# Post-LN decoder layer: values for eight heads at a time in twelve slots, v2 behind the first cross head, cross keys projected late in the self transposed stage

## The reference, cut to what matters

```python
x = layernorm(x + attn(x, w_qkv, w_proj, q_norm_w, k_norm_w))   # self: RMS norm and rotary on q, k; causal softmax
x = layernorm(x + xattn(x, ctx, ctx, mask, Wq, Wk, Wv, Wo))      # cross: keys and values from ctx, causal too
x = layernorm(x + ffn(x, ...))                                   # heavy (1024) and light (128) gelu branches, added
```

## Time and profile before

| | us |
|---|---|
| median of 3 runs | 953.05 (951.24 to 955.12) |
| the profiled execution, its own time | 952.55 |
| its span, first to last instruction | 950.8 |

### The profile page before, as it was taken

How to read it: one execution, slowest core, us unless ns; L and a number is a source line. 1 busy time by engine, 2 the same in 40 slices (tenths; PEclk the granted TensorE clock), 3 DMA queues, 4 the chain that set the end, 5 groups by cost and what they waited for, 6 DMA issues and landing times.

```text
span 950.8 us, 21384 instructions
## 1 busy us (share of the span) xinstructions
PE 852.0 (90%) x7381; PEld 649.0 (68%) x7381; DVE 720.1 (76%) x1765; ACT 632.8 (67%) x1404; POOL 538.7 (57%) x1047
## 2 busy tenths in 40 slices
PE   3367898999999999999999999999999999889887
PEld 2235565776867677776867676776867676657677
DVE  7788787787888878877888878877888879675522
ACT  1132453787878787787878778787878777776352
POOL 7554464656656574665756575655756665444143
PEclk8769898999999999999999999999999999999999
DMA  3794382845656382736676482826566472823101
GB/s 113 105 179 82 50 108 37 115 48 91 80 102 79 60 111 47 108 41 109 74 102 79 71 104 46 109 37 116 66 102 79 74 97 46 105 34 54 27 2 34
DMA packets 79660, 74.21 MB, mean 78 GB/s; under 512 B 8608, under 2 KB 78912, under 8 KB 79552
## 3 DMA queue, kind: packets, MB, share of 16 engines
q1 hardware_dynamic: 75024, 68.11, 50.7%
q10 hardware_dynamic: 4528, 4.73, 1.9%
HBM read 17.49 MB, written 4.20 MB: 23 GB/s over the span
## 4 chain that ended last, share of the span: by engine, by line
PE 60%; DVE 21%; ACT 5%; issue 5%; POOL 4%; DMA 3%; SPq 0%; ACTq 0%; POOLq 0%; DVEq 0%
PE bank L401 56%; DVE mx L1048 8%; PE bank L428 3%; POOL pr L1433 3%; DVE qn L1179 2%; ACT pr L854 2%; DVE x L1135 2%; ACT bank L788 1%; DMA stk2k<-nat1k 1%; POOL rstd L1412 1%; DVE y L1107 1%; DVE nt L1169 1%; ACT nat2q L788 1%; DVE rest L1022 1%; DVE st L1114 1%
## 5 line engine op out<-in xcount | busy, mean ns | idle before, releaser
L1433 POOL TENSOR_SCALAR_AFFINE_SELECT pr<-pr 128x256 f32<-128x256 f32 x512 | 223.1, 445 | 201.8 <-ACT pr L854 199.7
L854 ACT ACTIVATE pr<-bank 128x384 f32<-128x384 f32 x512 | 239.0, 495 | 138.2 <-PE bank L401 136.9
L1048 DVE TENSOR_REDUCE mx<-bank 128x3 f32<-128x384 f32 x512 | 264.5, 549 | 75.3 <-PE bank L401 70.6
L788 ACT ACTIVATE bank<-cmaskb 128x384 f32<-128x384 bf16 x331 | 155.0, 491 | 37.9 <-DVE mx L1048 33.0
L401 PE MATMUL bank<-w,g 128*128 128x256 f32 x576 | 171.2, 388 | 0.3 <-ACT g L874 0.3
L401 PE MATMUL bank<-stk2k,stk2q 97*128 97x128 bf16 (+1 forms) x512 | 87.2, 254 | 13.3 <-ACT bank L788 13.3
L401 PEld LDWEIGHTS bank<-w,g 128*128 128x128 f32 x576 | 89.3, 190 | 3.9 <-ACT g L874 0.7
L401 PE MATMUL bank<-stk1q,stk1k 100*128 100x256 bf16 (+1 forms) x512 | 79.2, 251 | 5.2 <-ACT pr L854 3.6
L874 ACT ACTIVATE g<-bank,b 128x256 f32<-128x256 f32 x144 | 65.1, 467 | 22.9 <-PE bank L401 22.9
L401 PE MATMUL bank<-stk1k,stk1q 97*128 97x128 bf16 (+1 forms) x512 | 75.4, 247 | 0.3 <-ACT bank L788 0.3
L401 PE MATMUL bank<-cmaskb,idb 128*128 128x256 bf16 x181 | 52.1, 288 | 25.0 <-DMA stk2k<-nat1k 13.9
(11 more groups left out here) (171 smaller groups left out, 1842.0 us busy)
## 6 DMA issues: line engine op xcount, KB each, us to landing
stk1q<-nat1q SPq DMA_DIRECT2D x90, 128.0 KB, 4.6
stk1k<-nat1k SPq DMA_DIRECT2D x90, 128.0 KB, 5.3
stk2k<-nat2k SPq DMA_DIRECT2D x90, 128.0 KB, 4.3
stk2q<-nat2q SPq DMA_DIRECT2D x90, 128.0 KB, 5.6
xT<-in_xT SPq DMA_DIRECT2D x16, 256.0 KB, 5.4
ctxT<-in_ctxT SPq DMA_DIRECT2D x16, 256.0 KB, 5.8
x<-in_x SPq DMA_DIRECT2D x16, 256.0 KB, 6.0
out_x<-x SPq DMA_DIRECT2D x15, 256.0 KB, 2.2
```

The source lines that it names most:

```text
L788: return nc.scalar.activation(out, in_, ACT.Copy)
L854: nc.scalar.activation(pr[:, h % (2 * HG), :], ring_bank("T", a, b, h)[:, 0:3 * P], ACT.Exp, scale=HD ** -0.5)\
L1048: V.tensor_reduce(mx3[:, h, :], scored[:, 0:3 * P].rearrange("p (k t) -> p k t", k=3), AX.X, ALU.max, negate=True).then_inc(s_mx[a], 1)
L1433: G.affine_select(out=slot, in_=slot, compare_op=ALU.is_ge, fill=0.0, base=0, pattern=[[0, 2], [1, P]], channel_multiplier=-1).then_inc(s_ ...
```

## The change

- `values` takes eight heads (half 0 or 1) instead of four: heads 0 to 3 of a half write columns 0 to 255 of bank 3, heads 4 to 7 columns 256 to 511. Half 0 stands at position 11 of its own stage, half 1 where group 3 stood. So there are four calls for each batch instead of eight, with the same matmuls.
- `pr` has 12 slots instead of 8, taken round all turns; `copy_half` copies 128 x 512 once where `copy_group` copied 128 x 256 twice. Half 0 is copied ahead of the exponential of head 12, half 1 where group 3 was.
- `k2` moves from position 1 of T2 to position 14 of T1, and ACT's high part of it from ahead of head 3 to ahead of head 0 of T2.
- `v2` moves from position 6 to position 1 of S2.
- `qr` becomes the same buffer as `qn`, and `scale_qk` waits for the transposes of the batch before instead of its rotation.

```diff
+NV = 2
+HV = H // NV
+SLOTS = 12
...
-        qn = sb("qn", [P, TT, 2 * D]); rot = sq; qc = sb("qc", [P, TT, 2 * D]); qr = sb("qr", [P, TT, 2 * D])
+        qn = sb("qn", [P, TT, 2 * D]); rot = sq; qc = sb("qc", [P, TT, 2 * D]); qr = qn
...
-        pr = sb("pr", [P, 2 * HG, 3 * P])
+        pr = sb("pr", [P, SLOTS, 3 * P])
...
+        def slot(a, b, h):
+            return (H * transposed.index((a, b)) + h) % SLOTS
...
-            def values(a, b, gr):
-                pe.wait_ge(s_prob[a], H * b + HG * (gr + 1))
-                if gr == 0:
+            def values(a, b, half):
+                pe.wait_ge(s_prob[a], H * b + HV * (half + 1))
+                if half == 0:
...
-                    pe.wait_ge(s_oT[a], NG * b + gr)
+                    pe.wait_ge(s_oT[a], NV * b + half)
                 v = values_of(a, b)
                 for key in range(2):
-                    for j in range(HG):
-                        h = HG * gr + j
-                        out = bank[OT_BANK][VW * j:VW * (j + 1), :]
+                    for j in range(HV):
+                        h = HV * half + j
+                        n = slot(a, b, h)
+                        out = bank[OT_BANK][VW * (j % HG):VW * (j % HG + 1), j // HG * T:(j // HG + 1) * T]
                         if key == 0:
-                            mm(out[:, 0:T], v[:, 0, h, :], pr[:, h % (2 * HG), 0:T], True, False, True)
+                            mm(out[:, 0:T], v[:, 0, h, :], pr[:, n, 0:T], j < HG, False, True)
...
                 if live(s):
-                    for gr in range(NG - 1):
-                        add(HG * gr + VALUES_AFTER, values, 1, s, gr)
+                    add(VALUES_AT, values, 1, s, 0)
+                    add(K2_AT, k2, s)
...
-                    add(K2_AT, k2, s)
-                    add(OUT1_AT[0], values, 1, s, NG - 1)
+                    add(OUT1_AT[0], values, 1, s, 1)
...
-                copy(oT[:, gr, :], bank[OT_BANK][:, 0:T]).then_inc(s_oT[a], 1)
+                copy(oT[:, PG * half:PG * (half + 1), :], bank[OT_BANK][:, :].rearrange("p (g t) -> p g t", g=PG))\
+                    .then_inc(s_oT[a], 1)
...
-                if h >= 2 * HG:
-                    act.wait_ge(s_pv[a], NG * b + h // HG - 1)
...
+                n = H * transposed.index((a, b)) + h - SLOTS
+                if n >= 0:
+                    a0, b0 = transposed[n // H]
+                    act.wait_ge(s_pv[a0], NV * b0 + n % H // HV + 1)
...
-                wait(dve, s_rope, TT * b)
+                wait(dve, s_nat[1], 2 * b)
...
-VALUES_AFTER = 7
+VALUES_AT = 11
-QKT_AT, MAX1_AT, V2_AT = 2, 4, 6
+QKT_AT, MAX1_AT, V2_AT = 2, 4, 1
-K2_AT, OUT1_AT, QK1_AT, V1_AT = 1, (3, 9), (3, 6), 13
+K2_AT, OUT1_AT, QK1_AT, V1_AT = 14, (3, 9), (3, 6), 13
-COPY1_AT, SQ_AT = (0, 3, 3), (5, 7)
+COPY1_AT, SQ_AT = (0, 0, 3), (5, 7)
```

More of the change, by code:

```diff
@@ L223, in build @@
                  if 0 <= turn[2] < B]
+        transposed = [turn[1:] for turn in turns if turn[0] == "T"]
+        def slot(a, b, h):
+            return (H * transposed.index((a, b)) + h) % SLOTS
         RING = (0, 1, 2)
@@ L581, in transpose_max @@
                     if live(b - 2):
-                        pe.wait_ge(s_oT[2], NG * (b - 1))
-                    wait(pe, s_oT[1], NG * b)
+                        pe.wait_ge(s_oT[2], NV * (b - 1))
+                    wait(pe, s_oT[1], NV * b)
                 for t in range(TT):
@@ L609, in values @@
                 else:
-                    pe.wait_ge(s_oT[a], NG * b + gr)
+                    pe.wait_ge(s_oT[a], NV * b + half)
                 v = values_of(a, b)
                 for key in range(2):
-                    for j in range(HG):
-                        h = HG * gr + j
-                        out = bank[OT_BANK][VW * j:VW * (j + 1), :]
+                    for j in range(HV):
+                        h = HV * half + j
+                        n = slot(a, b, h)
+                        out = bank[OT_BANK][VW * (j % HG):VW * (j % HG + 1), j // HG * T:(j // HG + 1) * T]
                         if key == 0:
-                            mm(out[:, 0:T], v[:, 0, h, :], pr[:, h % (2 * HG), 0:T], True, False, True)
+                            mm(out[:, 0:T], v[:, 0, h, :], pr[:, n, 0:T], j < HG, False, True)
                         else:
-                            last = mm(out[:, P:T], v[:, 1, h, :], pr[:, h % (2 * HG), T:3 * P], False, True, True)
+                            last = mm(out[:, P:T], v[:, 1, h, :], pr[:, n, T:3 * P], False, True, True)
                 last.then_inc(s_pv[a], 1)
             def out_tokens(b):
-                pe.wait_ge(s_oT[2], NG * (b + 1))
+                pe.wait_ge(s_oT[2], NV * (b + 1))
                 for t in range(TT):
@@ L711, in step @@
                 if live(f):
-                    add(OUT2_AT[0], values, 2, f, NG - 1)
+                    add(OUT2_AT[0], values, 2, f, 1)
                 if live(c):
@@ L775, in step @@
                 if live(c):
-                    for gr in range(NG - 1):
-                        add(HG * gr + VALUES_AFTER, values, 2, c, gr)
+                    add(VALUES_AT, values, 2, c, 0)
                 phase((lambda h: scores_t(2, c, h)) if live(c) else None, others)
@@ L791, in copy_v @@
                 act.wait_ge(s_v[a], b + 1)
-                wait(act, s_pv[a], NG * (b - 1) if a == 1 else NG * b)
+                wait(act, s_pv[a], NV * (b - 1) if a == 1 else NV * b)
                 copy(values_of(a, b)[:, :, :, 0:HD], bank[V_BANK[a]][:, :].rearrange("p (t h d) -> p t h d", t=TT, h=H))\
@@ L804, in copy_out, with copy_half @@
                 copy_dims(onT[2], dim_bank(b)).then_inc(s_onT[2], 1)
-            def copy_group(a, b, gr):
-                act.wait_ge(s_pv[a], NG * b + gr + 1)
+            def copy_half(a, b, half):
+                act.wait_ge(s_pv[a], NV * b + half + 1)
                 if a == 1:
@@ L812, in copy_group @@
                 elif live(b + 1):
-                    act.wait_ge(s_tok, C * (b + 1) + gr // PG + 1)
+                    act.wait_ge(s_tok, C * (b + 1) + half + 1)
                 else:
                     wait(act, s_ott, TT * b)
-                copy(oT[:, gr, :], bank[OT_BANK][:, 0:T]).then_inc(s_oT[a], 1)
+                copy(oT[:, PG * half:PG * (half + 1), :], bank[OT_BANK][:, :].rearrange("p (g t) -> p g t", g=PG))\
+                    .then_inc(s_oT[a], 1)
             def copy_x1(b):
@@ L843, in exponential @@
                 act.wait_ge(s_st[a], H * b + h + 1)
-                if h >= 2 * HG:
-                    act.wait_ge(s_pv[a], NG * b + h // HG - 1)
[L847 to L854, removed]
+                n = H * transposed.index((a, b)) + h - SLOTS
+                if n >= 0:
+                    a0, b0 = transposed[n // H]
+                    act.wait_ge(s_pv[a0], NV * b0 + n % H // HV + 1)
+                nc.scalar.activation(pr[:, slot(a, b, h), :], ring_bank("T", a, b, h)[:, 0:3 * P], ACT.Exp, scale=HD ** -0.5)\
                     .then_inc(s_exp[a], 1)
@@ L938, in step @@
                     if live(s):
-                        if h % HG == 0 and h >= 2 * HG:
-                            copy_group(1, s, h // HG - 2)
+                        if h == SLOTS:
+                            copy_half(1, s, 0)
                         exponential(1, s, h)
@@ L956, in step @@
                     if live(c):
-                        if h % HG == 0 and h >= 2 * HG:
-                            copy_group(2, c, h // HG - 2)
+                        if h == SLOTS:
+                            copy_half(2, c, 0)
                         exponential(2, c, h)
@@ L1431, in mask_probs @@
                     wait_apart(pool, (s_exp[a], H * b + h + 1))
-                    slot = pr[:, h % (2 * HG), :].rearrange("p (k t) -> p k t", t=P)[:, 0:3:2, :]
-                    G.affine_select(out=slot, in_=slot, compare_op=ALU.is_ge, fill=0.0, base=0,
+                    probs = pr[:, slot(a, b, h), :].rearrange("p (k t) -> p k t", t=P)[:, 0:3:2, :]
+                    G.affine_select(out=probs, in_=probs, compare_op=ALU.is_ge, fill=0.0, base=0,
                                     pattern=[[0, 2], [1, P]], channel_multiplier=-1).then_inc(s_prob[a], 1)
```

16 lines of the change are left out of this document (6 added, 10 removed).

## The result

| | before | after |
|---|---|---|
| median of 4 runs each | 953.17 (951.24 to 955.12) | 964.57 (962.89 to 968.18) |
| the profiled execution, its own time | 952.55 | 968.18 |
| its span | 950.8 | 965.2 |

The ratio is 1.0125, with a 95% interval of 1.0087 to 1.0162: slower by more than the noise, and outside the range of the prediction, 942 to 963. The profiled execution is the slowest of the four of after, so the spans differ by 14.4 us where the medians differ by 11.4.

The account below looks back on a forecast made before the run. TensorE was taken to bound the kernel, but only where the chain is on it; POOL's rstd behind a mask held x1. 952.55 + 1.3 (steps) - 0.5 (start) + 0.3 (end) = 953.65, predicted 953.7 us, range 942 to 963.

Parts of the forecast that it names:

- The call of eight heads: TensorE's values call of eight heads lasts 1.44 us; four calls fewer for each batch save 0.96 us of TensorE.
- Rival (d): Heads 4 to 7 of a half restart the column groups, each call costs 0.24 more; 964 us; chance 0.06.
- T1 into T2: Boundary of T1 and T2: half 1 ends at 437.52 instead of 437.73, a gain of 0.21 us.
- rival (c): Boundary of T1 and T2 loses its cover, half 1 starts 0.83 later: +9.1, 963 us; chance 0.19.
- T2 to x1: End of T2: x1 transposes start at 449.34 instead of 449.56; from T1 to the transposes 0.22 us is gained.
- S1: Position 3 of S1 holds a double call: cost 0.52 us on TensorE, 0.44 after slack (0.36 to 0.65).
- S2: v2 fills idle at the second cross head, but ACT's list is full: gain 0.1 us, bounds 0 and 0.88.
- rival (a): The idle at the second cross head does come off the end, 0.88 instead of 0.10; 945 us; chance 0.18.
- The steps: Eleven equal steps: -0.22 + 0.44 - 0.10 = +0.12 us a step, +1.3 in all.
- Start and end: Pipeline start -0.5 us (bounds -2 and +1), end with the last batch's half 1 exposed +0.3 (bounds 0 and 0.9).

Follow-up runs that it names:

- e7: The changed kernel with POOL's rstd one place earlier, ahead of the mask of head 12 of T2; 952.26 us, ratio 0.9985 to the kernel before.
- e4: The kernel before with v2 at position 1 of S2 and nothing else; 954.55 us, ratio 1.0000.
- e5: The changed kernel with overwritten filler matmuls at 15 idle places of TensorE in steps 0 to 3, 14 and 15; 952.56 us, ratio 0.9984.
- e6: The kernel before with overwritten filler matmuls at 15 idle places of TensorE in steps 0 to 3, 14 and 15; 950.55 us, ratio 0.9967.
- e1: The changed kernel with calls of eight heads for batches 2 to 12 only, four heads in the others; 960.48 us, ratio 1.0067 to the kernel before.
- e2: The changed kernel with all values calls of four heads at the old positions, the rest of the change kept; 952.67 us, ratio 0.9993.

## Why the prediction was wrong

The forecast was 953.7, no change; measured were 964.6. Point by point:

- **The call of eight heads**: 1.44 predicted, 1.44 measured (458.00 to 459.44 below). Rival (d) falls.
- **T1 into T2**: 0.21 of gain predicted, 0.06 measured. Half 1 ends at 445.05; TensorE's first head of T1 stands at 431.64 where it stood at 424.26, so this is 437.67 in the time of before, against 437.73. It starts 0.05 behind the mask of head 15, as said (443.62; in the chain the two masks before it end at 442.55 + 1.02 = 443.57); the idle time is 0.36 ahead of it and 0.25 two heads earlier, by the rows. Not foreseen was that the mask of head 14 takes 0.65 instead of 0.41 (below). Of rival (c)'s two extra instructions none came.
- **T2 to x1**: from the start of half 1 to the transposes 13.26 predicted (449.34 - 436.08), 13.25 measured (456.87 - 443.62). The order (mask of head 12, rstd, x1) is as said, and so, nearly, is the idle time (1.2 predicted, 0.93 by the row); e7 shows that it was the bound.
- **S1**: +0.44 predicted, +0.45 measured, from the x1 transposes to the first cross head (420.28 - 403.43 = 16.85 for 412.76 - 396.36 = 16.40).
- **S2**: -0.10 predicted, -0.14 measured; the idle at the second cross head is gone and rival (a) with it: e4 gains 0.16 a step where 0.88 was idle. ACT is what took its place: in e4's chain of waits S2 runs through ACT's table load, copies and biases.
- **The steps**: the sum was +0.12 and came to +0.24, all of the difference at the boundary of T1 and T2.
- **Start and end**: this is the step that failed, +6.0 for -0.5 and +5.8 for +0.3, outside the bounds that I had given them. Both terms were sums of durations taken at a granted clock of 1.00, and put TensorE's clock at nothing without a reason. I had read the clock only for the steps, and never asked whether the change makes idle time in the thin parts of the pipeline, or makes slow time there cost more. e5 and e6 show that with the clock held the two terms are -1.1 and +0.3. Rivals (c), 963, and (d), 964, lie near the measured time by chance: neither mechanism took place.

The rows behind the first two points, PE of after:

```profile
443.62 1.51 PE L409 MATMUL bank<-pr,va1b 128*32 128x256 f32 x32 [0.36 <-POOL pr L1432]
445.05 0.72 PE L409 MATMUL bank<-wqk1high,xThigh 128*128 128x512 f32 x2
...
458.00 1.51 PE L409 MATMUL bank<-pr,va 128*32 128x256 f32 x32
459.44 0.28 PE L409 MATMUL bank<-cmaskb,idb 128*128 128x256 bf16 x1
```

## What to carry to other kernels

A sum of durations holds only at the clock at which its rows were taken: read the granted clock of every stretch, fill and drain too, and ask of a change that merges waits what it does to the idle stretches there. Drains saved on TensorE are worth nothing where the chain leaves it; here one constant that moved a small instruction ahead of a mask on POOL's list brought 7.6 us in the kernel before, and 0.81 a step in the changed one, where the old order had turned saved time into idle time. Where TensorE must wait in a thin part, overwritten products that keep its clock up can pay.

## What the hardware showed that I had not expected

**TensorE's clock falls between short waits.** In the drain of after the clock fell within an idle stretch of 1.48 us, behind 4.40 us in which TensorE was busy 3.48, and it cost 1.28 on one call alone (2.72 for 1.44). Fillers in the idle time kept it at 2.4 GHz in the drain and took 12.0 us off one kernel and 3.5 off the other. The idle stretches alone do not foretell a fall: e1 fell behind ones that e2 has too, and e2 kept 1.00. The Trainium skill (TensorE: Matmul & The Clock Gate, A second HAM failure mode: psum-queue depth-cycling) tells of a kernel whose short idle times between groups of matmuls send the clock to and fro; these rows agree, in the two ends of a kernel that keeps 1.00 in all its middle.

**POOL's masks take longer beside some instructions of DVE.** A mask takes 0.41 alone. Beside DVE's product of two SBUF operands it took 0.65. At the start, beside the splitting of the weights (a cast, then a subtraction), one mask took 1.52, and this and the next together 4.20: the first row below is the first mask, the second row is both. POOL and then DVE of after:

```profile
64.13 1.52 POOL L1432 TENSOR_SCALAR_AFFINE_SELECT pr<-pr 128x256 f32<-128x256 f32 x1
...
64.13 4.20 POOL L1432 TENSOR_SCALAR_AFFINE_SELECT pr<-pr 128x256 f32<-128x256 f32 x2
...
441.81 0.41 POOL L1432 TENSOR_SCALAR_AFFINE_SELECT pr<-pr 128x256 f32<-128x256 f32 x1
...
442.55 0.65 POOL L1432 TENSOR_SCALAR_AFFINE_SELECT pr<-pr 128x256 f32<-128x256 f32 x1 [0.33 <-ACT pr L857]
```
```profile
63.94 1.45 DVE L1194 CAST w1h<-g 128x2304 fp32r<-128x2304 f32 x1
...
65.42 2.64 DVE L1196 TENSOR_TENSOR w1l<-g,w1h 128x2304 fp32r<-128x2304 f32 x1
...
442.51 0.43 DVE L1083 TENSOR_TENSOR on<-tok,rden 128x256 f32<-128x256 f32 x1
```

Each of the three masks ends 0.26 or 0.27 behind the instruction of DVE that started just before it or while it waited: 65.65 behind 63.94 + 1.45 = 65.39, 68.33 behind 65.42 + 2.64 = 68.06, and 443.20 behind 442.51 + 0.43 = 442.94. The Trainium skill (SBUF — State Buffer, Who interferes with whom) says that a DVE instruction with two SBUF inputs contends with a GpSimd instruction that reads SBUF, and the one that comes second is blocked; the rows of the product and of the subtraction agree. The cast has one SBUF input, so that sentence does not cover the mask beside it. In the first batch the call of eight heads waits 4.56 us behind such masks. No experiment took DVE's instruction away from beside a mask, so the 0.65 is read from rows and not shown by a run.
